# Four layers of a graph kernel on one core: row broadcasts by transfers, no negated means, layer two's slope and mask on VectorE, a new order of steps

## What is computed

```python
# x: (32, 256, 128) f32, adj: (32, 256, 256) int32, 0 or 1; no weights are shared between layers
# layer 1, attention by two scores a node
Wh = x @ W0.T;  s1 = Wh @ a1;  s2 = Wh @ a2
e = leaky_relu(s1[:, :, None] + s2[:, None, :], 0.2)
x = layernorm(x + softmax(where(adj == 0, -inf, e)) @ Wh)
# layer 2, attention by a bilinear form
h = x @ W1;  z = Ax.T + Ay + (h @ a_12) @ h.T
att = softmax(where(adj > 0, leaky_relu(z, 0.2), -9e15))
x = layernorm(x + elu(x @ W_1 + (att @ x) @ W_2))
# layer 3, four heads of 32
att = softmax(where(adj | eye, q @ k.T * scale, lowest), per head)
x = layernorm(x + relu((att @ v) @ Wo + bo))
# layer 4, a gated sum over the relation with number 1
vals = (x @ W_loop.T + b) * sigmoid(x @ W_loop.T @ Wg_loop.T + bg)
x = layernorm(x + relu((adj == 1) @ vals))
```

## Time and profile before

| what | us |
|---|---|
| median of 3 runs | 498.07 (496.0 to 498.63) |
| the profiled execution, its time | 496.9 |
| its span, first to last instruction | 495.0 |
| PE busy in the span | 468.4 (95%) |
| ACT busy | 428.0 (86%) |
| DVE busy | 410.8 (83%) |
| POOL busy | 370.6 (75%) |

### The profile page before, as it was taken

The page is one execution under the profiler, slowest core; times in us unless marked ns, Lnnn a source line. Parts: engine busy times, 40 slices in busy tenths (PEclk is TensorE's granted clock), DMA queues, the critical chain, the costliest instruction groups (busy, mean ns, idle before and its releaser), DMA issues. The chain is left out here.

```text
span 495.0 us, 13988 instructions
## 1 busy us (share of the span) xinstructions
PE 468.4 (95%) x3872; PEld 402.3 (81%) x3872; DVE 410.8 (83%) x1605; ACT 428.0 (86%) x1261; POOL 370.6 (75%) x736
## 2 busy tenths in 40 slices
PE   6968999999999999999999999999999999999793
PEld 5756778988888888988888888888888888877572
DVE  5657898998888998898888988898898989876653
ACT  3558999999999999999999999999999999988750
POOL 1365576788888888888888888888888888986523
PEclk9989999999999999999999999999999999999997
DMA  7211111122112221222112221221123100000011
GB/s 219 74 44 44 44 54 52 40 63 66 40 48 66 66 66 54 54 66 63 36 56 66 65 60 51 66 65 43 45 66 87 34 23 13 23 24 23 22 45 44
DMA packets 40222, 26.93 MB, mean 54 GB/s; under 512 B 2641, under 2 KB 39889, under 8 KB 40146
## 3 DMA queue, kind: packets, MB, share of 16 engines
q1 hardware_dynamic: 40146, 26.03, 18.4%
HBM read 17.63 MB, written 8.39 MB: 53 GB/s over the span
## 5 line engine op out<-in xcount | busy, mean ns | idle before, releaser
L1211 POOL TENSOR_SCALAR x<-y,minus_mean,rstd 128x128 f32<-128x128 f32 x244 | 144.8, 601 | 6.8 <-issue 5.1
L788 ACT ACTIVATE p<-p,nmax 128x256 f32<-128x256 f32 x256 | 128.5, 530 | 0.4 <-DVE nmax L981 0.4
L981 DVE CUSTOM_DVE_ANT_0 p<-ps,neg 128x256 f32<-128x256 f32 x256 | 90.7, 420 | 2.3 <-PE ps L564 2.3
L1193 POOL TENSOR_TENSOR rstd<-ve,minus_half 128x2 f32<-128x2 f32 x128 | 91.1, 712 | 0.0
L575 PE MATMUL ps<-ident,p 128*128 128x128 f32 x512 | 78.0, 275 | 4.1 <-DVE nmax L981 3.4
L1186 POOL TENSOR_SCALAR ve<-stats 128x2 f32<-128x2 f32 x128 | 24.6, 192 | 72.3 <-DVE stats L896 64.9
L797 ACT COPY p2T<-ps 128x512 f32<-128x512 f32 x128 | 75.2, 590 | 1.3 <-PE ps L575 0.5
L575 PEld LDWEIGHTS ps<-ident,p 128*128 128x128 f32 x512 | 61.3, 143 | 9.3 <-DVE nmax L981 4.0
L788 ACT ACTIVATION_READ_ACCUMULATOR p<-p,nmax 128x1 f32 x256 | 56.1, 219 | 0.0
L896 DVE BATCH_NORM_STATS2 stats<-y 128x6 f32<-128x256 f32 x128 | 54.1, 423 | 1.5
L1175 POOL TENSOR_TENSOR relu<-relu,neg 128x512 f32<-128x512 f32 x32 | 37.1, 1161 | 21.1 <-ACT relu L757 21.1
(11 more groups left out here) (130 smaller groups left out, 1210.3 us busy)
## 6 DMA issues: line engine op xcount, KB each, us to landing
adj_in<-in_adj_dram SPq DMA_DIRECT2D x32, 256.0 KB, 3.0
xT<-in_xT_dram SPq DMA_DIRECT2D x32, 128.0 KB, 2.1
x_in<-in_x_dram SPq DMA_DIRECT2D x32, 128.0 KB, 2.1
x_aside<-x SPq DMA_DIRECT2D x32, 128.0 KB, 2.1
...
l_w<-in_l_w_dram SPq DMA_DIRECT2D x1, 256.0 KB
...
```

Source lines behind the costliest of these rows:

```text
L788: last = nc.scalar.activation(p2(n)[:, k, a, :], p2(n)[:, k, a, :], ACT.Exp, bias=nmax2(n)[:, k, a:a + 1], scale=-1.0, accum_out=sum2(n)[: ...
L981: last = nc.vector.tensor_tensor_reduce(p2(n)[:, k, a, :], bank("sc2", n, a)[:, k * N:(k + 1) * N], neg2(n)[:, k, :], -1.0, HIGHEST, ALU.a ...
L1193: nc.gpsimd.tensor_tensor(rstd[layer](n), ve[layer](n), minus_half[:, :], ALU.pow)\
L1211: last = nc.gpsimd.tensor_scalar(dst[:, k, 0:D], y_t[layer](n)[:, k, :], minus_mean[layer](n)[:, k:k + 1], rstd[layer](n)[:, k:k + 1], ALU ...
```

## The change

- s2: for graphs 3 to 31, PE's s2_rows and ACT's c_s2 are gone. proj0 makes one more column, 0.2 times the score s2, SP's s2_out writes the two columns s2 and 0.2 s2 to DRAM (256 nodes x 8 bytes), and s2_in reads them back to all 128 partitions (2 KB each). s2row holds both, interleaved, and e0 reads both from there. Graphs 0 to 2 go as before.
- rs: rs_rep is gone. rs_rows transposes the 128 x 8 reciprocals in one transpose, c_rs copies 8 x 128 to SBUF, and SP's rs_in spreads each of the 8 rows over 32 partitions in two transfers.
- The negated mean is gone; norm and end_norm subtract the mean from the statistics.
- Layer two: relu1 writes 0.2 z by a copy with a scale; lk1, new on DVE, takes the maximum of z and that, one instruction of 128 x 512; e1 adds neg1 (now unscaled) and finds maxima from two SBUF tensors; rmask1 is gone. z1's bank is freed by lk1 instead of e1.
- All places in PLAN are new. xw0 has 4 buffers instead of 3, s2row 3 instead of 2. The flag's steps on PE and DVE move behind the last graph's work.

```diff
...
-    "sync": [("ld_xT", 6707), ("ld_adj", 7906), ("ld_w", 8043), ("ld_x", 8602), ("aside", 16291), ("store", 19013)],
-    "tensor": [("proj0", 8774), ("s2_rows", 9402), ("prep_a", 11038), ("pT0", 11053), ("prep_c", 11151),
-        ("agg0", 11161), ("prep_d", 11846), ("prep_b", 12046), ("xT1", 12143), ("tT", 12198), ("z1", 12448),
-        ("xw1", 12450), ("pT1", 12863), ("flag", 13095), ("agg1", 13150), ("xT2", 13535), ("qk2", 13667),
-        ("sc2", 13818), ("pT2b0", 14335), ("pT2a0", 14520), ("pT2a1", 14582), ("rs_rows", 15014), ("v2", 15091),
-        ("pT2b1", 15180), ("agg2", 15365), ("wo2", 15578), ("xT3", 16401), ("hg3", 16731), ("agg3", 17296)],
-    "scalar": [("c_proj0", 8986), ("c_s2", 9439), ("exp0", 10878), ("c_prep_a", 10907), ("c_pT0", 11066),
-        ("c_prep_c", 11302), ("c_prep_d", 11955), ("c_xT1", 12119), ("c_prep_b", 12238), ("c_tT", 12318),
-        ("relu1", 12513), ("c_xw1", 12553), ("exp1", 12734), ("c_pT1", 13058), ("c_elu1", 13159), ("c_xT2", 13557),
-        ("c_qk2", 13730), ("exp2b", 14126), ("exp2a", 14363), ("c_pT2b0", 14524), ("c_pT2a0", 14709),
-        ("c_pT2a1", 14722), ("c_rs", 15060), ("c_v2", 15069), ("c_pT2b1", 15262), ("c_xT3", 16468), ("gate3", 16807)],
-    "vector": [("masks", 9611), ("e0", 9640), ("m0", 10555), ("eq1", 10747), ("neg1", 10779), ("s0", 11213),
-        ("r0", 11373), ("y0", 11444), ("b0", 11520), ("flag_a", 11952), ("e1", 12743), ("r1", 13069), ("h1", 13108),
-        ("y1a", 13200), ("y1b", 13267), ("b1", 13417), ("flag_b", 13435), ("e2b", 14017), ("e2a", 14038),
-        ("r2", 14743), ("onT2", 15553), ("y2a", 15795), ("y2b", 15854), ("b2", 15915), ("end_norm2", 16376),
-        ("vals3", 16995), ("y3", 17485), ("b3", 17599), ("end_norm3", 18642)],
-    "gpsimd": [("var0", 11545), ("rsq0", 11592), ("norm0", 12023), ("neg2", 12065), ("rmask1", 12520),
-        ("var1", 13324), ("rsq1", 13342), ("norm1", 13471), ("rs_rep", 14753), ("var2", 16029), ("rsq2", 16104),
-        ("norm2", 16213), ("var3", 18121), ("rsq3", 18145), ("norm3", 18673)],
+    "sync": [("ld_xT", 6088), ("ld_adj", 7356), ("ld_w", 7679), ("s2_out", 8058), ("s2_in", 8685), ("ld_x", 9444),
+        ("rs_in", 14882), ("aside", 17971), ("store", 19680)],
+    "tensor": [("proj0", 7553), ("s2_rows", 9322), ("prep_a", 10454), ("pT0", 10786), ("prep_c", 11131),
+        ("agg0", 11196), ("prep_d", 11322), ("prep_b", 11356), ("xT1", 11888), ("tT", 12115), ("z1", 12355),
+        ("xw1", 12360), ("pT1", 12900), ("agg1", 13156), ("xT2", 13452), ("qk2", 13614), ("sc2", 13859),
+        ("v2", 14010), ("pT2b0", 14347), ("pT2a1", 14418), ("pT2a0", 14424), ("rs_rows", 14636), ("pT2b1", 15268),
+        ("agg2", 15366), ("wo2", 15687), ("xT3", 16913), ("hg3", 17285), ("agg3", 17552), ("flag", 21518)],
+    "scalar": [("c_proj0", 7671), ("c_s2", 9479), ("exp0", 10398), ("c_prep_a", 10780), ("c_pT0", 10950),
+        ("c_prep_c", 11266), ("c_prep_b", 11515), ("c_prep_d", 11834), ("c_xT1", 11998), ("c_tT", 12173),
+        ("relu1", 12365), ("c_xw1", 12401), ("exp1", 12878), ("c_pT1", 13084), ("c_elu1", 13202), ("c_xT2", 13513),
+        ("c_qk2", 13816), ("c_v2", 14111), ("exp2b", 14115), ("exp2a", 14235), ("c_pT2b0", 14262),
+        ("c_pT2a1", 14621), ("c_pT2a0", 14737), ("c_rs", 14893), ("c_pT2b1", 15229), ("c_xT3", 17091),
+        ("gate3", 17247)],
+    "vector": [("masks", 9360), ("neg1", 9929), ("e0", 9983), ("m0", 10287), ("eq1", 10877), ("s0", 11313),
+        ("r0", 11379), ("y0", 11428), ("b0", 11638), ("lk1", 12762), ("e1", 12830), ("flag_a", 13032), ("r1", 13063),
+        ("h1", 13066), ("y1a", 13141), ("y1b", 13220), ("b1", 13256), ("e2b", 14050), ("e2a", 14052), ("r2", 14800),
+        ("onT2", 15803), ("y2a", 15946), ("y2b", 16115), ("b2", 16193), ("end_norm2", 16580), ("vals3", 17489),
+        ("y3", 17860), ("b3", 18387), ("end_norm3", 19477), ("flag_b", 28425)],
+    "gpsimd": [("var0", 11550), ("rsq0", 11585), ("norm0", 11859), ("neg2", 11905), ("var1", 13260), ("rsq1", 13316),
+        ("norm1", 13338), ("var2", 16218), ("rsq2", 16471), ("norm2", 16885), ("var3", 18574), ("rsq3", 19019),
+        ("norm3", 19031)],
...
-    "adj": 5, "x": 3, "xT0": 2, "neg0": 3, "neg1": 3, "neg2": 6, "eq1": 7, "xw0": 3, "s2row": 2, "p0": 2, "p0T": 2,
+    "adj": 5, "x": 3, "xT0": 2, "neg0": 3, "neg1": 3, "neg2": 6, "eq1": 7, "xw0": 4, "s2row": 3, "p0": 2, "p0T": 2,
...
+PE_ROWS = 3
...
     **{step: (-1, 0) for step in ("flag_a", "flag", "flag_b")},
+    **{step: (0, PE_ROWS) for step in ("s2_rows", "c_s2")},
+    **{step: (PE_ROWS, 0) for step in ("s2_out", "s2_in")},
...
-    "z1": [("b", "e1_ready")],
+    "z1": [("b", "leaky_ready")],
...
-        s2row = ring("s2row", [N])
+        s2row = ring("s2row", [N, 2])
...
-        rs_rep = ring("rs_rep", [T, D], of="rs_row")
+        rs_turned = ring("rs_turned", [P], of="rs_row")
...
+            def rs_in(n):
+                sp.wait_ge(sem("rs_sb"), n + 1)
+                free(sp, "rs_row", n, "onT_sb")
+                for k in range(T):
+                    sp.dma_start(rs_row(n)[:, k * P:(k + 1) * P],
+                                 rs_turned(n)[k * HEADS:(k + 1) * HEADS].rearrange("h (a i) -> h a i", a=1)
+                                 .broadcast_to((HEADS, DK, P))).then_inc(sem(f"rs_in{n % RING['rs_row']}"), 16)
+
+            def s2_out(n):
+                sp.wait_ge(sem("wh_sb"), n + 1)
+                sp.dma_start(s2_dram[n].rearrange("(t p) c -> p t c", p=P), xw0(n)[:, :, 1:3])\
+                    .then_inc(sem(f"s2_out{n % 2}"), 16)
+
+            def s2_in(n):
+                sp.wait_ge(sem(f"s2_out{n % 2}"), 16 * ((n - PE_ROWS) // 2) + 16)
+                free(sp, "s2row", n, "e0_ready")
+                sp.dma_start(s2row(n).rearrange("p j c -> p (j c)"),
+                             s2_dram[n].rearrange("(a j) c -> a (j c)", a=1).broadcast_to((P, 2 * N)))\
+                    .then_inc(sem(f"s2_in{n % RING['s2row']}"), 16)
...
             def rs_rows(n):
                 o = bank("rs_rows", n)
                 bank_free(pe, "rs_rows", n)
-                pe.wait_ge(sem("rs_rep_ready"), n + 1)
-                for k in range(T):
-                    last = pe.transpose(o[:, k * P:(k + 1) * P], rs_rep(n)[:, k, :], ident[:, :])
-                last.then_inc(sem("rs_ps"), 1)
+                pe.wait_ge(sem("rsum2_ready"), n + 1)
+                pe.transpose(o[0:T * HEADS, 0:P], rsum2(n).rearrange("p t h -> p (t h)"), ident[:, :])\
+                    .then_inc(sem("rs_ps"), 1)
...
-                nc.scalar.copy(w0_w[:, 1:2], ps[:, 0, 1:2]).then_inc(sem("weights_ready"), 1)
+                nc.scalar.copy(w0_w[:, 1:2], ps[:, 0, 1:2])
+                nc.scalar.mul(w0_w[:, 2:3], ps[:, 0, 2:3], SLOPE).then_inc(sem("weights_ready"), 1)
...
             def c_rs(n):
                 act.wait_ge(sem("rs_ps"), n + 1)
-                free(act, "rs_row", n, "onT_sb")
-                nc.scalar.copy(rs_row(n), bank("rs_rows", n)[:, 0:N]).then_inc(sem("rs_sb"), 1)
+                if n >= RING["rs_row"]:
+                    act.wait_ge(sem(f"rs_in{n % RING['rs_row']}"), 16 * T * (n // RING["rs_row"]))
+                rows = slice(0, T * HEADS)
+                nc.scalar.copy(rs_turned(n)[rows, :], bank("rs_rows", n)[rows, 0:P]).then_inc(sem("rs_sb"), 1)
...
-                nc.scalar.activation(relu(n).rearrange("p t n -> p (t n)"), bank("z1", n), ACT.Relu,
-                                     scale=(1.0 - SLOPE) / SLOPE).then_inc(sem("relu_ready"), 1)
+                nc.scalar.activation(relu(n).rearrange("p t n -> p (t n)"), bank("z1", n), ACT.Copy,
+                                     scale=SLOPE).then_inc(sem("relu_ready"), 1)
...
             def neg1_(n):
                 dve.wait_ge(sem(f"adj_loaded{n % RING['adj']}"), 16 * (n // RING["adj"]) + 16)
-                free(dve, "neg1", n, "rmask_ready")
-                nc.vector.tensor_scalar(neg1(n), adj_in(n), 0.0, NEG_L1 / SLOPE, ALU.is_le, ALU.mult)\
+                free(dve, "neg1", n, "e1_ready")
+                nc.vector.tensor_scalar(neg1(n), adj_in(n), 0.0, NEG_L1, ALU.is_le, ALU.mult)\
...
             def e0(n):
-                dve.wait_ge(sem("s2_sb"), n + 1)
+                if n < PE_ROWS:
+                    dve.wait_ge(sem("s2_sb"), n + 1)
+                    row = bank("s2_rows", n)[:, 0:N]
+                else:
+                    dve.wait_ge(sem(f"s2_in{n % RING['s2row']}"), 16 * ((n - PE_ROWS) // RING["s2row"]) + 16)
+                    row = s2row(n)[:, :, 0]
                 free(dve, "p0", n, "pT_ps0")
                 for k in range(T):
-                    last = nc.vector.scalar_tensor_tensor(out=p0(n)[:, k, :], in0=bank("s2_rows", n)[:, 0:N],
-                                                              scalar=xw0(n)[:, k, 0:1], in1=s2row(n),
-                                                              op0=ALU.add, op1=ALU.max)
```

(41 more changed lines are left out.)

41 lines of the change are left out of this document (21 added, 20 removed).

## The result

The changed kernel takes 512.06 us in the median (510.85 to 512.42), beside 497.03 us (495.13 to 498.63) of the kernel before on the same chip: a ratio of 1.030, with a 95% interval of 1.025 to 1.035. It is slower by 15 us, where I had forecast 490.5 us and a range up to 499. The profiled execution has a span of 508.4 us.

What follows compares the result with a forecast made beforehand. PE was taken to bound the body, with no gap in its 14.00 us round. Body 6.4, other rounds and head chain 1.5, tail 0.3, head's order -0.6: together 7.6 us off, median 498.07 to 490.5 us, range 485 to 499.

Steps and rivals of the forecast that it cites:

- PE's round of 13.68 us: TensorE in the body: broadcasts leaving it take 0.21 and 0.11 us off its 14.00 us round.
- Part 3: POOL and the negated means: 2.5 us a round leave POOL, no body gain, x1 to x4 some 0.2 us earlier each.
- Part 4: New order, laid out with old durations: PE has every operand 0.2 us or more ahead; head some 0.6 us later.
- the forecast 13.75: Body round in us, taken because DVE with 13.67 us of work and one gap can't follow 13.68 exactly.
- The transfers in the body: Four more transfers a round on SP's queue, covered by the plan's places: nothing; s2_out landing under 5 us.
- The tail: After the last graphs: rs_in takes about 3 us, onT2 starts over a us sooner: nothing; without minus_mean 0.3 us gained.
- that term: Head's order: pT0 of graph 0 waits for graph 3 too, some 0.6 us later.
- level with PE: DVE's round in the body: 13.67 us occupied, ends 12.91 and 14.43, beside PE's 13.68; busy 13.3 to 13.6.
- Rival (d): e0 on DVE at half pace with two f32 SBUF operands: 14.19 us a round, 503 us; chance 0.03.
- my upper end of 0.16 us a collision: DVE's two e0 and two e1 a round each cost 0 to 0.16 us more beside POOL's SBUF work; 0.06 taken.
- (c): Wait inside DVE's loop, r1 for agg1 or y1b for the exponential: 14.20 us a round, 503 us; chance 0.10.
- (a): PE takes everything: DVE under 13.5 us, no wait left, all 9.6 us come, 486 to 488 us; chance 0.18.

Runs made afterwards that it cites:

- n1: The changed kernel with GpSimd's normalisation adding the mean instead of subtracting it (values wrong): 492.02 us, ratio 0.989.
- n2: The changed kernel with the negated mean and the addition in the normalisation restored: 495.04 us, ratio 0.997.
- n9: n2 with the rs_in transfer for graphs 0 to 28 and the old path of the reciprocals' rows for the last three: 487.76 us, ratio 0.981.
- n5: n2 with the reciprocals' rows made as before (POOL's copy, two transposes, ACT's copy, no rs_in): 492.05 us, ratio 0.989.
- n7: n5 with PE's s2_rows back for all graphs, leaving only lk1 and the new order: 502.65 us, ratio 1.011.
- n3: The kernel before with only the negated mean taken out, so the normalisation subtracts: 497.93 us, ratio 1.002.
- n6: The changed kernel, subtraction kept, with xT3, hg3 and c_xT3 moved later in the round: 500.24 us, ratio 1.007.

## Why the prediction was wrong, step by step

**PE's round of 13.68 us was right.** n1, n2 and n9 have 13.67 or 13.68, n5 has 0.11 more, n7 has 14.00 or more. Both prices, 0.21 and 0.11 us, come out as taken.

**Part 3 is the step that failed.** "POOL isn't the bound, so the body gains nothing; x1 to x4 come some 0.2 us earlier each" counted the instructions that leave POOL and priced none that changes. The normalisation's operation was altered by the diff, 244 times, and its row was on the page and in no group of mine. Rather than 0.2 us earlier, x3 comes late: norm1, norm0 and norm2 stand between layer two's statistics and x3, six instructions of 912 ns instead of n1's 525, 2.3 us of the 3.1 that this stretch of POOL has grown. I should have bounded the change of operation from both sides, as for lk1.

**Part 4 failed with it.** The order was laid out "with the old durations", and the finding was that PE has every operand 0.2 us or more ahead. x3 wasn't among the tight ones: in n1 it has 2.4 us before xT3. But six instructions of one kind stand before it, and a duration wrong by 0.39 us counts six times. The layout was never asked which lead goes if a duration is wrong; n3 and n6 show that the same slow instruction costs nothing, or little, in an order with room. For the order itself (n1, n2, n9) the forecast 13.75 was 0.07 too high.

**The transfers in the body: right by their cover.** s2_out was to land in under 5 us; the page of the changed kernel has 6.3:

```profile
adj_in<-in_adj_dram SPq DMA_DIRECT2D x32, 256.0 KB, 5.6
s2row<-s_rows SPq DMA_DIRECT2D x29, 256.0 KB, 4.3
xT<-in_xT_dram SPq DMA_DIRECT2D x32, 128.0 KB, 5.4
...
x_aside<-x SPq DMA_DIRECT2D x32, 128.0 KB, 7.8
...
s_rows<-xw SPq DMA_DIRECT2D x29, 2.0 KB, 6.3
```

All stays within the places that the plan gives, and no round waits for it.

**The tail was mis-sized.** "Nothing" was 8 to 9 us. rs_in of the last graph was taken at about 3 us, which no row of such a transfer backed (the 3.0 of the earlier trace rows are a plain load's), and takes 6.5; that onT2 "starts over a us sooner" can't help when its operand is the transfer. The halved clock behind the wait was in no term. In the head the changed kernel needs 1.1 us more until graph 0's sc2 (40.3 against 39.2), n9 39.1 and n2, with the same head, 40.1: what is left of that term can't be told from zero. PE's longest wait before, 2.5 us by the prediction, is 2.7 us (L387, in the setup at the start), which changes nothing.

**DVE.** It didn't come level with PE: in n9 it is busy 330.23 of 360 us, 12.5 us a round of 13.68, where 13.3 to 13.6 were to show the forecast right. The sum took every old duration as given, and y2b's median fell from 585 ns to 416. As for lk1, it has a median of 691 ns and holds DVE 0.61 us from start to start (0.59 forecast). The kernel's e0 and e1 by themselves (min/median/max in ns), changed kernel:

```profile
L937 DVE SCALAR_TENSOR_TENSOR p<-s2row,xw x58: 468/482/1452, 27.6 to 419.6; 128x256 f32<-128x256 f32 x58
...
L982 DVE CUSTOM_DVE_ANT_0 p<-relu,neg x64: 412/418/535, 25.6 to 457.3; 128x256 f32<-128x256 f32 x64
```

Against means of 473 and 422 before that is nearly nothing, in the mean too (506 and 422). Rival (d), e0 at half pace, is contradicted, and with it the Trainium skill's rule (page "Vector Engine (DVE) Microarchitecture Reference", section "Points that are easy to get wrong"): 482 ns isn't 740. But the maximum of 1452 ns breaks my upper end of 0.16 us a collision. In n1_norm_add that happens often (e0's mean is 683 ns there, with a median of 475); one round of DVE's and of POOL's timeline:

```profile
211.14 1.58 DVE L937 SCALAR_TENSOR_TENSOR p<-s2row,xw 128x256 f32<-128x256 f32 x2
```

```profile
210.89 1.15 POOL L1210 TENSOR_TENSOR neg<-neg,not_eye 128x512 bf16<-128x512 bf16 x1
```

POOL's instruction ends at 212.04. The first e0 takes 1.18 us, to 212.32, and the second 0.47, so the first took 0.7 us more than alone. In n1 all 18 e0 that start during this instruction of POOL (neg2, two SBUF inputs) take 0.98 to 1.40 us, and the 23 that start during its power of -0.5 at most 0.48; in the changed kernel the 56 that start during the normalisation have a median of some 482 ns and a maximum of 602. So the exclusion that the Trainium skill (page "SBUF — State Buffer", section "Who interferes with whom") states, and that I had set aside for the smaller additions in the rows, shows beside one kind of POOL's instructions and not beside the two others. It didn't decide: with DVE at 13.76 of 14.00 us n1 still has PE's round.

**The rivals.** None was this one: all put the new wait on DVE, ACT or SP. (c) had the right form, a wait inside a loop while PE holds work, at the wrong engine. (a), PE takes everything with 486 to 488, is what n9 shows (487.76) once the two faults are away. In sum: the span was to be 487.4; n9's is 485.9; the slow subtraction with too tight an order adds 508.4 - 494.6 = 13.8 us, and the last graphs' transfer 494.6 - 485.9 = 8.7 us.
